# First attention: where SyncE stores a finished result among its other transfers

## What is computed

```python
q = _rmsnorm(x @ wq_a.T, q_a_ln_w) @ wq_b.T
...
ckv, k_pe = (ckv_kpe[..., :KVR], ckv_kpe[..., KVR:])
kv = _rmsnorm(ckv, kv_a_ln_w) @ wkv_b.T
...
scores = jnp.einsum('bqhd,bkhd->bhqk', q_full, k_full) * softmax_scale
causal = jnp.tril(jnp.ones((S, S), dtype=bool))
scores = jnp.where(causal[None, None], scores, jnp.finfo(scores.dtype).min)
attn = jax.nn.softmax(scores, axis=-1)
out = jnp.einsum('bhqk,bkhd->bqhd', attn, v).reshape(B, S, H * VD)
return out @ wo.T
```

## Time and profile before

| | us |
|---|---|
| runs of the kernel before, median of 3 | 2767.33 |
| lowest and highest of them | 2752.13, 2769.16 |
| the profiled execution, its own time | 2770.99 |
| its span, first to last instruction | 2769.2 |
| PE busy in the span | 2229.6 |
| DVE busy | 1196.6 |
| ACT busy | 871.1 |
| POOL busy | 238.5 |

### The profile page before, as it was taken

How to read it: one execution, slowest core, us unless ns; L and a number is a source line. 1 busy time by engine, 2 the same in 40 slices (tenths; PEclk the granted TensorE clock), 3 DMA queues, 4 the chain that set the end, 5 groups by cost and what they waited for, 6 DMA issues and landing times. The chain is left out here.

```text
span 2769.2 us, 34091 instructions
## 1 busy us (share of the span) xinstructions
PE 2229.6 (81%) x12304; PEld 1253.3 (45%) x12304; DVE 1196.6 (43%) x3459; ACT 871.1 (31%) x1566; POOL 238.5 (9%) x181
## 2 busy tenths in 40 slices
PE   6354998898888888888886777736799999999678
PEld 5152555555555555555552434523444444444233
DVE  2043644443444444444401323322176767766055
ACT  0041233333333333333340101012135555555311
POOL 0002011111111111111100000000000000000100
PEclk7576799999999999999997989657758989989799
DMA  4612222222222221222204040323311222220211
GB/s 163 199 39 51 49 58 65 65 53 63 65 65 65 51 50 48 63 65 65 63 17 171 16 163 16 109 100 113 92 25 33 41 41 41 42 40 19 85 59 67
DMA packets 96346, 186.73 MB, mean 67 GB/s; under 512 B 26442, under 2 KB 33482, under 8 KB 95986
## 3 DMA queue, kind: packets, MB, share of 16 engines
q1 hardware_dynamic: 96178, 184.56, 25.0%
HBM read 97.45 MB, written 30.93 MB: 46 GB/s over the span
## 5 line engine op out<-in xcount | busy, mean ns | idle before, releaser
L693 ACT ACTIVATE at_prob<-at_scp 128x512 f32<-128x512 f32 (+1 forms) x608 | 346.9, 577 | 630.1 <-PE at_scp L796 619.8
L1357 ACT ACTIVATE as_prob<-as_scp 128x1024 f32<-128x1024 f32 (+3 forms) x384 | 306.4, 810 | 239.5 <-PE as_scp L1448 176.8
L727 DVE CUSTOM_DVE_ANT_0 at_junk<-at_mxp,causal 128x128 f32<-128x128 f32 (+3 forms) x512 | 241.9, 486 | 306.1 <-PE at_mxp L805 294.2
L1460 PE MATMUL as_mxp<-l_keys,as_q 48*128 48x512 f32 (+2 forms) x768 | 300.0, 488 | 57.1 <-DVE as_mxf L1404 19.5
L805 PE MATMUL at_mxp<-l_khi,at_qhi 96*128 96x512 f32 (+2 forms) x768 | 307.0, 440 | 34.5 <-DVE at_tm L751 16.7
L792 PE MATMUL at_scp<-at_qhi,l_khi 97*128 97x512 f32 (+1 forms) x608 | 250.7, 412 | 70.5 <-ACT at_prob L693 67.8
L1409 DVE CUSTOM_DVE_ANT_0 as_junk<-as_mxp,causal 128x384 f32<-128x384 f32 (+3 forms) x512 | 228.2, 487 | 99.3 <-PE as_mxp L1460 96.5
L795 PE MATMUL at_scp<-at_qlo,l_khi 96*128 96x512 f32 (+1 forms) x608 | 237.8, 391 | 0.0
L796 PE MATMUL at_scp<-at_qhi,l_klo 96*128 96x512 f32 (+1 forms) x608 | 236.3, 389 | 0.0
L1460 PEld LDWEIGHTS as_mxp<-l_keys,as_q 48*128 48x128 f32 x768 | 133.4, 202 | 223.0 <-DVE as_mxf L1404 80.2
L1442 PE MATMUL as_scp<-as_q,l_keys 49*128 49x512 f32 (+2 forms) x768 | 218.8, 412 | 6.1 <-ACT as_prob L1357 6.0
(11 more groups left out here) (195 smaller groups left out, 2564.6 us busy)
## 6 DMA issues: line engine op xcount, KB each, us to landing
at_qhi<-at_shi SPq DMA_DIRECT2D x192, 128.0 KB, 2.4
at_qlo<-at_slo SPq DMA_DIRECT2D x192, 128.0 KB, 2.4
m_w<-in_wmod SPq DMA_DIRECT2D x12, 1024.0 KB, 10.8
jw_wo<-in_wo_t SPq DMA_DIRECT2D x8, 1024.0 KB, 8.1
at_spread<-l_recips SPq DMA_DIRECT2D x64, 128.0 KB, 2.8
l_o<-at_u_sb SPq DMA_DIRECT2D x16, 512.0 KB, 3.5
as_q<-scratch_queries SPq DMA_DIRECT2D x48, 128.0 KB, 4.8
as_q<-l_queries_b SPq DMA_DIRECT2D x48, 128.0 KB, 4.3
```

The source lines that it names most:

```text
L693: nc.scalar.activation(prob[:, x % RING0, c0:HALF], scp[x % BANKS0][:, c0:HALF], ACT.Exp).then_inc(s["exp_done"], 1)
L727: nc.vector.tensor_tensor_reduce(out=junk[:, u % 2, 0:w], in0=tile[:, 0:w], in1=k.causal[:, HALF - w:HALF], scale=1.0, scalar=LOWEST, op0= ...
L1357: nc.scalar.activation(prob[:, r:r + 2, c0:HALF], scp[p % 2][:, :, c0:HALF], ACT.Exp).then_inc(s["exp_done"], 1)
L1460: nc.tensor.matmul(mxp[banks["max", u][0]][:, 0:w], q[t % SLOTS1][rows, j // 2, qt * P:(qt + 1) * P], k.keys[rows, t // NG, k0:k0 + w], st ...
```

## The change

In SP's loop, `outcome(t - 2)` moves from behind `results(t - 1)` to right behind `queries(t + 1)`, ahead of `weights(t + 2)`. No instruction is added or dropped, and the waits inside the functions stay. What follows the loop is as it was.

```diff
                 for t in range(STEPS0):
                     if t + 1 < STEPS0:
                         queries(t + 1)
+                    if t >= 2:
+                        outcome(t - 2)
                     if t + 2 < STEPS0:
                         weights(t + 2)
                     if t >= 1:
                         results(t - 1)
-                    if t >= 2:
-                        outcome(t - 2)
                     if t + 1 < STEPS0:
                         maxima_row(t + 1)
```

## The result

The changed kernel takes 2664.19 us in the median of four runs (2652.76 to 2669.01); the kernel before took 2764.14 us in the median of the four runs beside it (2752.13 to 2769.16). The ratio is 0.9636, 95% interval 0.9607 to 0.9665: faster by 3.6%. The forecast was 2664.5 us.

A forecast was written before the change was run, and what follows sets the result against it. PE was taken as the bound once its stall for the store goes. 2770.99 - 108.0 (stall) + 3.4 (late weights) = 2666.4 us; from the median, 2662.7; the middle, 2664.5 us, was forecast, range 2643 to 2697.

The forecast's parts named there:

- The stall and its size: First attention: ACT's wait for the result store and PE's pause go, 99.48 us in steps 2 to 13, 8.5 in step 14.
- Conditions of the moved store: SP's queue: the store waits only for POOL's earlier normalisation, costs SP nothing, and lands 19 us before ACT wants it.
- The weights behind the store: Projections in steps 2 to 13: weights land later behind the moved store and stall PE, 3.4 us in all.
- D: Lateness of the weights' landing caused by the moved store, costing what exceeds each step's slack; taken as 1.8 us.
- The argument that these stalls leave the clock alone: First attention: short waits in step 1 leave TensorE's clock at 1.00, so weight stalls up to 1.07 us shouldn't lower it.
- signs of being right: Among them: steps 2 to 13 of 66.6 to 67.7 us at clock 1.00, line 834 weight waits of 0 to 1.5 us.
- The upper bound of 29.8 us: Steps 2 to 13: most that late weights cost if their transfer begins only after the slowest store, 4.1 us.
- The bound of 1.5 us for D: Least lateness of the weights if their signal can't come before the slowest store is through: 4.1 - 2.6 us.
- The weights rival: Steps 2 to 13: weights' lateness near its upper bound, time 2691 us; chance 0.12.
- A clock that takes its share elsewhere: TensorE falls to the lower clock in other places, only 67.8 us idle time returns, about 2701 us; chance 0.09.
- That the change does nothing: ACT waits on for something that comes with the last step's results; time stays at 2767 us; chance 0.04.
- the slower case: Weights land 15.2 us after issue, 14.0 us lost in each of 12 steps, time 2827 us; chance 0.02.

The follow-up runs named there:

- the changed kernel again: The changed kernel run once more with no edit, for its spread: 2666.02 us, ratio 0.9655 to the kernel before.

## Why the prediction was right, and where it was not

**The stall and its size: right.** A free step takes 66.7 us in the mean in the kernels without a stall, as the pattern of step 1 said. Gross I had 99.48 us for steps 2 to 13 and 8.5 for step 14. With the weights out of the way they came to 898.80 - 800.16 = 98.6 us and 66.12 - 57.49 = 8.6, together 107.3 against 108.0. Pricing the slow stretch behind the pause with the pause was needed: idle time alone was 67.8 us of it.

**Conditions of the moved store: right.** SP goes from the queries to the store with no gap (645.20 + 7.54 = 652.74, then 652.78), and ACT asks for it long after it has landed.

**The weights behind the store: the mechanism right, its size off.** The term was 3.4 us and measured 10.9 in the first profile, and 9.1 and 7.5 in the two others of the same kernel (809.34 less 12 x 66.69, 807.57 less 12 x 66.67). The median was well guessed: the issue is 0.63 us later (652.78 to 653.41; I had 0.46) and the landing 0.9 us longer, D = 1.5 where I took 1.8. The failure lies in taking one D for all steps. In steps 7 to 13 of the first profile, where the weights land in 3.4 to 3.5 us, 2.5 us were lost (469.00 less 7 x 66.64), and the prediction has 2.9 of its 3.4 us there. In steps 2 to 6 it has 0.5 us, and 8.4 were lost (341.57 less 5 x 66.64): there the landing runs up to 5.6 us, which makes D 3.6 against a slack of 0.7 to 2.4 us. Nor were the paused steps the forecast ones: 3, 7, 8, 9 and 11 were named, 3, 4, 5, 8 and 9 paused.

The argument that these stalls leave the clock alone held for the sizes that it was made for, up to 1.07 us: no pause for the weights of 1.42 us or less lowered the clock in any trace. The pauses got longer than that. In step 3 one of 1.45 us and in step 5 one of 2.06 us were followed by a slow stretch, and the steps lost 2.4 and 4.5 us. Two of the signs of being right failed with them: steps of 66.6 to 67.7 us at clock 1.00, and waits of at most 1.5 us. The upper bound of 29.8 us held.

By the Trainium skill, DMA: Bandwidth & Descriptors, section "Queues, rings and completion order", a transfer's signal lands only after the earlier writes of its DMA engine. The traces agree: with the store ahead, the weights land after it in all 60 steps of the five executions. The bound of 1.5 us for D was worked out with a store of 4.1 us; the slowest one ahead of the weights in the first profile took 3.5, and the same working gives 0.9. That the median D is also 1.5 is not a confirmation of that number.

**The sum: nearer than its terms.** In the first attention I had 104.6 us net, and the profile shows (898.80 - 810.57) + (66.12 - 57.52) = 96.8. The span fell by 102.1 (2769.2 to 2667.1). The rest came from behind the last mark, 1372.5 us before and 1366.8 after, with 0.4 us lost ahead of the steps. That part isn't touched by the change, and it varies by more than this. So that forecast and measured median lie only 0.3 us apart is chance; an honest reading is a term missed by 4 to 8 us.

**The rivals.** The weights rival happened at 7.5 to 10.9 us of its 29.8. A clock that takes its share elsewhere in this attention is excluded by the kernel with the weights first, at 1.00 in all steps. That the change does nothing is excluded by the missing wait, and the slower case by landings of at most 5.6 us, where it needed 10.

## What to carry to other kernels

A store that has long been ready should not queue behind a wait for another engine; look at what its issuing engine waits for between the moment the data is ready and the issue. When it is moved up, look at what then stands right behind it and how much slack that has in its worst step, not in the mean: a load needed in the same step goes ahead of it, or the store goes to a place with nothing tight behind. In this kernel four other cures (weights first, store behind the sums' reload, store first of all, a third buffer) each take 800 to 801 us for steps 2 to 13 where the change takes 808 to 811.

## What the runs showed of the hardware

**The second layer's attention carries much of the spread of the whole.** Two kernels whose first attention agreed to 0.5 us differed by 26.5 us in their profiled executions. In the windows of equal length over the second layer's attention, first of the kernel with the weights first, then of the one with the store ahead of the queries, the granted clock differs, with the same instructions:

```profile
1950.30:2495.30 545.00, 508.09 (x3816) 242.24 (x3819) 342.88 (x1154) 302.40 (x407) 34.45 (x15) 0.84 0.20 35
```

```profile
1947.00:2492.00 545.00, 489.64 (x3926) 231.97 (x3926) 344.80 (x1160) 310.20 (x418) 35.55 (x15) 0.91 0.20 36
```

The first gets through 3816 matmuls in 545 us and the second through 3926. The spans behind the last mark were 1387.4 and 1364.9 us (2677.7 - 1290.3, 2651.9 - 1287.0). In the same window, 660 us behind the last mark, the ten profiled executions without the old stall read 0.84 to 0.91: the two lowest (0.84, 0.85) took 2680.84 and 2681.74 us, the two of 0.91 took 2654.35 and 2663.58, and the six others 2663.97 to 2676.06. That is likely what hides the 7 to 11 us which the cures gain in the first attention. It was measured only as a difference of clocks; what sets the clock there was not tried.

**A pause can be paid twice, and a short one too.** The pauses of 5.2 us (kernel before) and of 2.8 us (store before the spreading), both means, were followed by a stretch at 1.2 GHz in all of their 13 steps, which cost 3.1 and 2.4 us more. One pause of 2.8 us was followed by full speed first and by the slow stretch a microsecond later. For shorter pauses the length does not decide. The pause of 2.06 us cost 2.4 us more (4.5 us over a free step less 2.06). Here are step 3 of the first profile and step 3 of the changed kernel again:

```profile
521.25 1.25 PE L834 MATMUL at_mxp<-l_qa_t,at_wq 128*128 128x512 f32 x2 [1.45 <-DMA at_wq<-scratch_wq]
```

```profile
525.30 1.12 PE L834 MATMUL at_mxp<-l_qa_t,at_wq 128*128 128x512 f32 x2 [1.77 <-DMA at_wq<-scratch_wq]
```

The granted clock of the first step is 0.98, that of the second 1.00. Of the seven pauses of 1.45 to 2.06 us for the weights in all traces, those of 1.45, 1.79 and 2.06 us were followed by a slow stretch, and those of 1.48, 1.56, 1.77 and 1.86 us were not. What decides between them stays open.
